# Row copies to bf16 moved into the edge stage, and six thresholds formed beside the operand halves

## The reference, cut to what matters

```python
# layer 0: attention with 4 heads
ht = (h @ Wm).reshape(n, 4, 64)
scores = leaky_relu(el[:, :, None] + er.T[None, :, :], 0.2)      # masked by adj
out = einsum('nhj,jhf->nhf', softmax(scores), ht)
# layer 1: two GRU cells (edge, node) and 3 attention heads
node_support = adj_without_diagonal @ h
edge_output = gru_cell(node_support, h, ...)
att = where(adj_without_diagonal > 0, e_plus, NEG_INF)           # softmax over each row
edge_support = mean over heads of (softmax(att) * adj) @ (h @ W[i])
node_output = gru_cell(edge_support, h, ...)
# layer 2: neighbour mean and a linear layer; layer 3: a weight that is zero unless adj < 1 and not 0
```

## Time and profile before

| | us |
|---|---|
| median of 3 executions | 1327.91 (1324.97 to 1328.03) |
| the profiled execution's own time | 1326.06 |
| its span in the profile | 1324.0 |
| PE busy | 1139.3 (86%) |
| DVE busy | 937.4 (71%) |
| ACT busy | 784.3 (59%) |
| POOL busy | 228.1 (17%) |
| granted clock of TensorE, mean | 0.94 |
| layer 0's matmuls (L1620) | from 93.0 to 387.1 |

### The profile page before, as it was taken

How to read it: one execution, slowest core, us unless ns; L and a number is a source line. 1 busy time by engine, 2 the same in 40 slices (tenths; PEclk the granted TensorE clock), 3 DMA queues, 4 the chain that set the end, 5 groups by cost and what they waited for, 6 DMA issues and landing times.

```text
span 1324.0 us, 35106 instructions
## 1 busy us (share of the span) xinstructions
PE 1139.3 (86%) x15054; PEld 937.7 (71%) x15054; DVE 937.4 (71%) x2037; ACT 784.3 (59%) x1001; POOL 228.1 (17%) x296
## 2 busy tenths in 40 slices
PE   4519898888866989999978999999999997778997
PEld 3418898888865766666656888888888654446886
DVE  5786677767995299999986998769995365553541
ACT  3479988778825123333327999989989365653000
POOL 5631011111103012222222000001220141220000
PEclk9759899999995889999989999999999998999999
DMA  9936567879518334433337345318852000020532
GB/s 217 179 52 68 63 73 115 117 108 133 71 3 293 101 100 124 116 114 111 106 111 223 106 143 197 114 59 294 286 186 104 5 29 17 16 96 1 189 118 87
DMA packets 128083, 153.77 MB, mean 116 GB/s; under 512 B 32065, under 2 KB 105393, under 8 KB 127665
## 3 DMA queue, kind: packets, MB, share of 16 engines
q1 hardware_dynamic: 74993, 127.05, 30.4%
q0 software_dynamic: 51744, 23.88, 15.8%
q10 hardware_dynamic: 1184, 0.53, 0.1%
HBM read 171.26 MB, written 35.60 MB: 156 GB/s over the span
## 4 chain that ended last, share of the span: by engine, by line
PE 54%; DVE 23%; issue 8%; ACT 6%; POOL 4%; DMA 3%; SPq 0%; DVEq 0%; POOLq 0%; ACTq 0%
PE PS L1620 18%; PE PS L1761 10%; PE PS L1762 9%; DVE scratch L1317 9%; PE PS L1815 8%; PE PS L1711 3%; POOL arena L704 2%; PE PS L1802 2%; DVE arena L1299 2%; DVE arena L1091 2%; PE PS L1718 1%; DVE arena L1343 1%; PE PS L1655 1%; DMA arena<-e_rows 1%; DMA arena<-in_edge_WhhT 1%
## 5 line engine op out<-in xcount | busy, mean ns | idle before, releaser
L1761 PE MATMUL PS<-arena 128*128 128x257 f16 x1452 | 325.3, 272 | 7.0 <-ACT arena L898 4.1
L1762 PE MATMUL PS<-arena 128*128 128x257 f16 x1452 | 325.3, 274 | 0.0
L1620 PE MATMUL PS<-arena 128*128 128x65 f16 x7744 | 260.1, 196 | 74.7 <-DVE arena L1137 40.4
L1620 PEld LDWEIGHTS PS<-arena 128*128 128x128 fp8e4 x7744 | 256.7, 99 | 78.0 <-issue 77.4
L812 ACT ACTIVATE arena<-arena 128x1408 fp8e4<-128x1408 f32 x176 | 241.9, 1456 | 45.9 <-DVE arena L1131 45.7
L1317 DVE CUSTOM_DVE_ANT_0 scratch<-arena 128x1408 bf16<-128x1408 bf16 x132 | 223.1, 1690 | 23.2 <-DMA arena<-e_rows 10.8
L898 ACT ACTIVATE arena<-arena 128x896 int16<-128x896 uint8 (+1 forms) x198 | 187.0, 971 | 22.1 <-DVE arena L1372 14.2
L1761 PEld LDWEIGHTS PS<-arena 128*128 128x128 bf16 x1452 | 142.7, 98 | 31.0 <-issue 8.2
L1762 PEld LDWEIGHTS PS<-arena 128*128 128x128 bf16 x1452 | 139.9, 96 | 21.5
L1131 DVE TENSOR_TENSOR arena<-arena,AT 128x352 int32<-128x352 int32 x176 | 91.2, 518 | 78.0 <-PE PS L1620 59.7
L889 ACT ACTIVATE arena<-arena,E1B 128x896 uint8<-128x896 f32 (+1 forms) x131 | 139.1, 1063 | 1.7 <-DMA arena<-m_rows 1.7
(11 more groups left out here) (189 smaller groups left out, 1338.3 us busy)
## 6 DMA issues: line engine op xcount, KB each, us to landing
arena<-adj_rows_half SPq DMA_DIRECT2D x88, 352.0 KB, 3.0
arena<-in_adj SPq DMA_DIRECT2D x44, 704.0 KB, 4.4
adj_rows_half<-in_adj POOLq DMA_DIRECT2D x22, 704.0 KB, 11.9
hw_saved<-arena SPq DMA_DIRECT2D x22, 387.0 KB, 4.2
AT<-in_adjT POOLq DMA_DIRECT2D x44, 176.0 KB, 8.3
arena<-hw_saved SPq DMA_DIRECT2D x9, 774.0 KB, 6.6
arena<-el_rows SPq DMA_DIRECT2D x8, 704.0 KB, 10.3
arena<-h_saved SPq DMA_DIRECT2D x44, 128.0 KB, 2.1
```

The source lines that it names most:

```text
L1620: ins = pe.matmul(PS[:, first_bank(n) + i, (2 * r + q) * C0:(2 * r + q + 1) * C0], MASK[:, (m + j) % NMASK, q, k * P:(k + 1) * P], MOV[:, ...
L1761: pe.matmul(PS[:, k, 0:D + 1], weights, w[:, 0:D + 1], start=(j == 0), stop=False)
L1762: ins = pe.matmul(PS[:, k, 0:D + 1], weights, w[:, D + 2:2 * D + 3], start=False, stop=(j == NT - 1))
```

## The change

The row copies leave layer 0. Copies 0 to 3 are issued by GpSimd in the h loop at blocks 12, 15, 18 and 21, copy 4 after it, and copy t + 5 at the head of round t of the edge stage. Three may be in flight: each waits for the one three before. A copy is cut into quarters of a row in place of eighths. The single diagonal DMA becomes 22 DMAs of 128 elements, issued by SyncE when the copy has landed, four ahead of the edge stage and the others one in a round, after that round's half rows. SyncE waits for an earlier diagonal before half rows are loaded. On ScalarE, the first six thresholds are formed inside the loop that makes MOV, one in each of its rounds 14 to 19. NOTI becomes bf16, and the zeros ZB get a tile of their own.

```diff
+    THR_AT = 14
+    ROWS_LEAD = 5
-        NOTI = sb("NOTI", [P, P])
+        NOTI = sb("NOTI", [P, P], BF16)
+        ZB = sb("ZB", [P, 2], BF16)
+        copy_sems = [("adj_a", NT), ("adj_b", NT), ("rows_h", 0)]
+        def row_copied(t):
+            name, before = copy_sems[t % 3]
+            return sem(name), 16 * (before + t // 3 + 1)
 # SyncE
-            sp.wait_ge(sem("rows_h"), 16 * NT)
-            sp.dma_start(AH_D.rearrange("t p n -> (t p n)")[0:(P - 1) * NT * (N + 1)]
-                         .rearrange("(a b c) -> a b c", b=NT, c=N + 1)[:, :, 0:1],
-                         ZB[0:P - 1, :].unsqueeze(2), allow_slow_non_contiguous=True).then_inc(sem("rows_z"), 16)
-            sp.wait_ge(sem("rows_z"), 16)
+            def clear_diagonal(t):
+                n = P if t < NT - 1 else P - 1
+                sp.wait_ge(*row_copied(t))
+                sp.dma_start(AH_D.rearrange("t p n -> (t p n)")[t * P * (N + 1):(t * P + n) * (N + 1)]
+                             .rearrange("(a c) -> a c", c=N + 1)[:, 0:1],
+                             ZB[0:n, 0:1], allow_slow_non_contiguous=True).then_inc(sem("rows_z"), 16)
...
+            for t in range(ROWS_LEAD - 1):
+                clear_diagonal(t)
+            sp.wait_ge(sem("rows_z"), 16 * (ROWS_LEAD - 1))
             for L in range(2):
                 load_row(L)
...
                 if t + 2 < NT:
                     load_h(t + 2, HR, 0)
+                if 1 <= t and t + ROWS_LEAD - 2 < NT:
+                    sp.wait_ge(sem("rows_z"), 16 * (t + ROWS_LEAD - 1))
                 for L in range(loads_before(t + 1) if t else 2, loads_before(t + 2)):
                     load_row(L)
+                if t + ROWS_LEAD - 1 < NT:
+                    clear_diagonal(t + ROWS_LEAD - 1)
 # GpSimd
-            for t in range(NT):
-                pool.wait_ge(sem("masks_built"), 68 + 4 * t)
-                pool.dma_start(AH_D[t].rearrange("p (c n) -> c p n", c=8),
-                               t_in["adj"][t * P:(t + 1) * P, :].rearrange("p (c n) -> c p n", c=8)).then_inc(sem("rows_h"), 16)
+            def copy_row(t):
+                if t >= 3:
+                    pool.wait_ge(*row_copied(t - 3))
+                pool.dma_start(AH_D[t].rearrange("p (c n) -> c p n", c=4),
+                               t_in["adj"][t * P:(t + 1) * P, :].rearrange("p (c n) -> c p n", c=4)
+                               ).then_inc(row_copied(t)[0], 16)
             for t in range(NT):
                 pool.wait_ge(sem("h1"), t + 1)
                 pool.tensor_copy(HHL[:, t, 0, :], H32R[:, t % 8, :]).then_inc(sem("hi1"), 1)
+                if t >= 12 and t % 3 == 0:
+                    copy_row(t // 3 - 4)
+            copy_row(ROWS_LEAD - 1)
...
             for t in range(NT + 1):
+                if t + ROWS_LEAD < NT:
+                    copy_row(t + ROWS_LEAD)
                 if t < NT:
                     delta(t, 0, HR, GT)
 # ScalarE
             for t in range(NT):
                 act.wait_ge(sem("t_b"), t + 1)
                 act.wait_ge(sem("t_d"), t + 1)
                 act.activation(MOV[:, t, :, 0, :], TS[:, t % 3, :].rearrange("p (h c) -> p h c", c=C0), ACT.Copy
                                ).then_inc(sem("mov_hi"), 1)
+                if t == THR_AT:
+                    act.wait_ge(sem("u_mm"), 1)
+                    act.wait_ge(sem("elb0"), 16)
+                if THR_AT <= t < THR_AT + NTHR:
+                    threshold(0, t - THR_AT)
-            act.wait_ge(sem("mov"), NT)
-            act.wait_ge(sem("u_mm"), 1)
             for n, (g, h) in enumerate(units0):
                 act.wait_ge(sem(f"elb{n % 2}"), 16 * (n // 2 + 1))
                 for j in range(NT):
-                    threshold(n, j)
+                    if n > 0 or j >= NTHR:
+                        threshold(n, j)
```

More of the change, by code:

```diff
@@ L158, in gnn_stack_kernel @@
         RD = a0.take(11)
-        ZB = a0.take(NT, dt=BF16, size=2)
         NOTB = a0.take(P, dt=FP8, size=1)
@@ L168, in gnn_stack_kernel @@
         HTF = AT[:, :, htf_at:htf_at + 4 * H0 * C0].bitcast(F32)
-        assert NREAL <= (P - 1) * NT
         THRi = THR.bitcast(mybir.dt.int32)
@@ L540, in _ @@
                     load_h(t + 2, HR, 0)
+                if 1 <= t and t + ROWS_LEAD - 2 < NT:
+                    sp.wait_ge(sem("rows_z"), 16 * (t + ROWS_LEAD - 1))
                 for L in range(loads_before(t + 1) if t else 2, loads_before(t + 2)):
+                    assert half_of(L)[0] <= t + ROWS_LEAD - 2 or t + ROWS_LEAD - 2 >= NT - 1
                     load_row(L)
+                if t + ROWS_LEAD - 1 < NT:
+                    clear_diagonal(t + ROWS_LEAD - 1)
                 if t == NT - 2:
@@ L654, in _ @@
             pool.memset(ALR, 0.0).then_inc(sem("consts"), 1)
-            link(pool.memset(ZB, 0.0))
+            link(pool.memset(ZB[:], 0.0))
             pool.memset(ET[:], 1.0).then_inc(sem("consts"), 1)
@@ L799, in _ @@
             act.wait_ge(sem("coef"), 1)
-            for t in range(NT):
-                act.wait_ge(sem("t_b"), t + 1)
-                act.wait_ge(sem("t_d"), t + 1)
-                act.activation(MOV[:, t, :, 0, :], TS[:, t % 3, :].rearrange("p (h c) -> p h c", c=C0), ACT.Copy
-                               ).then_inc(sem("mov_hi"), 1)
             def threshold(n, j):
@@ L813, in threshold @@
                                bias=ERB[:, j, h:h + 1], scale=SHARP, saturate=False).then_inc(sem("t_act"), 1)
-            act.wait_ge(sem("mov"), NT)
-            act.wait_ge(sem("u_mm"), 1)
+            for t in range(NT):
+                act.wait_ge(sem("t_b"), t + 1)
+                act.wait_ge(sem("t_d"), t + 1)
+                act.activation(MOV[:, t, :, 0, :], TS[:, t % 3, :].rearrange("p (h c) -> p h c", c=C0), ACT.Copy
+                               ).then_inc(sem("mov_hi"), 1)
+                if t == THR_AT:
[3 more added lines that the diff above has]
+                    threshold(0, t - THR_AT)
             for n, (g, h) in enumerate(units0):
```

## The result

The changed kernel takes **1342.88 us** (median of 4) against 1326.44 for the kernel before on the same chip: a ratio of 1.013 [1.0095, 1.0164]. It is slower where I forecast faster, and outside the range. Its profiled execution took 1341.17 us with a span of 1339.3.

What follows compares the result with a forecast made beforehand. TensorE was taken to bound layer 0, VectorE the edge stage. Terms -20.0 - 0.3 + 1.6 + 0.5 + 1.5 + 1.5 = -15.2 us from 1326.06 gave 1310.9, as a median 1312.7 us; range 1301 to 1327.

Steps and rivals of the forecast that it cites:

- the edge stage: Edge stage, VectorE the bound: some 17 copies beside the half rows' loads cost +1.5 us (0 to 12).
- mean spare time: Edge stage: of 5.4 us for each half-row load, some 2.9 are spare; each further microsecond of landing costs 42.
- the half rows come late: Rival, chance 0.10: in the edge stage copies stretch half-row landings and VectorE waits; landing in 7.1 us gives 1359 us.
- SyncE ahead of the edge stage: Before the edge stage: scores queue behind the late save of the turned h, +1.5 us (0 to 4).
- The edge stage's waits on SyncE: Edge stage: SyncE's waits for copies come late enough, 18 us against 12.5 of landing; diagonals are covered by idle time.
- Layer 0: Layer 0, TensorE the bound: without row copies 20.0 us of 25.5 us of gaps go (12.1 to 25.5).
- gaps over 3 us without copies: Sign of being wrong: TensorE gaps longer than 3 us remain though no copies run.
- Half the gaps stay: Rival, chance 0.18: in layer 0 el rows cause 13.4 us of gaps, only 12.1 go; 1320.6 us.
- another cause: Rival, chance 0.04: layer 0's gaps are TensorE's own fetch pace, so nothing goes and 4.8 us come; 1332.7 us.
- Six thresholds: Start, MOV loop: six thresholds on ScalarE there change the time by -0.3 us (-1.5 to +1.5).
- Tables go back and forth: Rival, chance 0.03: Copy and Sigmoid each need their own table, 14.1 us of loads before TensorE's start; 1326.8 us.
- The h loop and the score sums: Copy issues between casts cost +1.6 us (0 to 4); gaps beside copies in the score sums +0.5 (-2.3 to +4).

Runs made afterwards that it cites:

- e2: The changed kernel with only the cut of the copies changed, to eighths of a row in place of quarters: 1316.82 us, ratio 0.9896.
- e3: The changed kernel with only the cut of the copies changed, to sixteenths of a row in place of quarters: 1309.85 us, ratio 0.9846.
- e4: The changed kernel without the 22 diagonal DMAs and SyncE's waits for them; its waits for the copies stay: 1336.54 us, ratio 1.0038.
- e7: e3 with copies 0 to 4 spread thinly over layer 0 in place of the h loop: 1310.13 us, ratio 0.9838.
- e11: e7 with each copy as 128 whole rows in place of sixteenths: 1314.0 us, ratio 0.9884.
- e1: The kernel before with only the six thresholds moved into the MOV loop, row copies left in layer 0: 1327.55 us, ratio 0.9983.
- e5: The changed kernel with each copy as 128 whole rows, not cut into quarters: 1317.26 us, ratio 0.9906.

## Why the prediction was wrong

**The step that failed is the edge stage, taken at +1.5 with an upper bound of 12; it measured +28.4.** In it I wrote that copies in quarters cost "less in quarters", kept 12.5 us for their landing, and stretched the half row by the ratio of el rows beside copies and without, 12.9 to 9.2, which gave 1.3 us. All three came from copies in eighths. The cut was part of the change, and I priced it only in GpSimd's issue. With quarters the half row grows by 3.3 us (6.4 - 3.1) and not 1.3, which is past the 2.9 us of mean spare time; the rival *the half rows come late* then holds, the one I gave 0.10. Its own price, 42 us for each microsecond past the spare, gives (3.3 - 2.9) x 42 = 17, beside 6 for the diagonals: with 28.4 measured its order is right. The prediction even had the landing of 6.4 us among its cases, as the one that eats the whole gain. Even with eighths the term would have been +10.0 (e2), for a half row that grows by 2.5 us, less than the mean spare time of 2.9, for which the prediction shows no working. That the tightest spare time of 1.9 us counted there and not the mean fits this, but isn't shown. With sixteenths it is +4.6 (e3).

**SyncE ahead of the edge stage**, taken at +1.5 (0 to 4), measured +14.7. It is the same error a second time: two landings were put at 12.5 each, 25 us from copy 0 to copy 3; they took 22.3 and 18.9, 41.5 us. That the scores wait behind the turned h was seen. Of the 14.7 us, 6.7 are the later write of the scores and 8.0 its longer landing, 9.4 us in place of 1.4. In e3, with sixteenths, this stretch takes 13.1 us, as before.

**The edge stage's waits on SyncE** were called covered: 18 us of lead against 12.5 of landing. 22.1 is more than 18, and so SyncE's wait for a copy can stand ahead of the next half row. I had named this as what would make me wrong ("if SyncE's wait for a copy or a diagonal ends after its next half row is due"). From 455 us on its queue waits 9.6 us in 3 times for copies and 21.6 us in 12 times for diagonals. But e4, where the second kind is gone and 8.4 us of waits for copies stay, keeps 22 of the 28.4 us: most of the loss is the half rows' own landing.

**Layer 0**: right in mechanism and nearly in size. I took 20.0 of the 25.5 us of gaps behind 185 us as gone; 19.4 went, and 6.1 stay where I put 5.5. Over all of layer 0 it is 20.4. One of my signs of being wrong was gaps over 3 us without copies, and two are there, 3.8 and 3.4 us long; they lie ahead of 160 us, where the kernel before had no row copies either. A further 5.4 us lie in TensorE's busy time, which I hadn't foreseen, and whose cause the rows don't give (the granted clock rose from 0.96 to 0.97 in layer 0, 1% of 260 us). Half the gaps stay (0.18) fell, and so did *another cause* (0.04): they went as the copies went, in every kernel that took them out, and e7 and e11 brought some back. That these gaps are TensorE's code coming late remains a reading; what is shown is that copies cause them. The rule of the Trainium skill that fetch is hidden (Runtime: NRT & Kernel Launch, Instruction fetch mechanics) would have had nothing go; the trace doesn't agree, with 20.4 us of gaps gone.

**Six thresholds**: taken -0.3 (-1.5 to +1.5). The first matmul came 2.0 us earlier, and 1.5 in e1, but what the thresholds give is 0.8 and 1.2 us by the loop itself. The start of that loop moves from profile to profile, from 54.1 to 59.6 us over all these kernels, by more than the term. VectorE's last low half ended at 86.8, not 88.3: from round 15 on a low half took 0.70 us where it had taken 1.11. *Tables go back and forth* (0.03) fell: the rows show one load. The Trainium skill (ScalarE: Activation LUTs, Table sets: the hidden batching unit) says that copy is in every set; the trace agrees, with one table load of 1.28 us.

**The h loop and the score sums**: +1.6 and +0.5 forecast. From first to last cast the loop took 23.3 us against 22.1 (+1.2), the score sums 16.1 against 15.6 (+0.5), and the loop began 1.1 later after layer 0. A copy's issue took 1.15 us, though (I had 0.8), and 1.06 to 1.15 in the median for every cut from 2 to 16 pieces.

Had the forecast been for sixteenths, 1309.85 us would have lain 3 us from it, but in part by luck. Against the kernel before, e3's profile has +3.0 us ahead of layer 0, -31.7 in it, +5.9 up to the end of the score sums, -0.1 and +1.7 up to the third maximum and +4.6 up to the 88th, where I had -0.3, -20.0, +2.1, +1.5, 0 and +1.5. Layer 0 alone differs by 6 us among kernels whose program is the same there (268.4 in the changed kernel, 262.5 in e3). What holds is that the copies' leaving layer 0 carried the gain, and that one number in the diff took it away.

## What to carry to other kernels

Before a transfer is moved beside others, work out how many DMA engines it uses: its queue's share x 16 x the stretch, over the count and the landing. If that is close to the size of its outermost dimension, that dimension limits it; give it 16 entries, or the 128 rows, before anything else is judged, as a low mean DMA share says nothing about a few engines that are full. Then ask what waits behind it in the issuing queue: a landing longer than the lead turns into a wait ahead of a transfer that has nothing to do with it. And where a change moves and re-cuts at once, price the two apart; here the move with sixteenths was worth 1.5%, and quarters cost nearly 3% against that.

## What the runs showed of the hardware

- The same 704 KB copied and cast from DRAM to DRAM lands in 35.9, 22.1, 13.2 and 9.2 us in 2, 4, 8 and 16 pieces, and in 7.0 as 128 whole rows, beside the same work. Other transfers land later the fewer its pieces: a half row in 10.0, 6.4, 5.6, 4.0 and 3.3 us. Beside quarters it is the last quarter of a half row's packets that is late, beside eighths the last half.
- GpSimd's issue of a copy takes 1.06 to 1.15 us in the median, in 2 to 16 pieces, and 0.55 as whole rows.
- Beside copies in packets of 22528 bytes (2.0 us each) saves of h on another queue took up to 15.7 us (e5), beside packets of 1408 bytes up to 10.1.
- A subtraction on VectorE (128x520, f32 to f16) took 1.11 us beside GpSimd's multiply and 0.70 where GpSimd stood idle, in the same loop.
